# Recommendation tower in fp32: another order of the first loads, the row groups, the dense part and layer 3

## What is computed

```python
e = stack([tbl_f[ids[:, f]] for f in range(26)], axis=1)          # 512 x 26 x 128
combined = concatenate([dense[:, None, :], e], axis=1)            # 512 x 27 x 128
interactions = einsum('bfd,bgd->bfg', combined, combined)
z = concatenate([dense, interactions[:, iu, ju]], axis=1)         # 128 + 351
h = concatenate([z, dense], axis=1)
h = maximum(h @ W_top1 + b_top1, 0.0)                             # 607 -> 512
h = maximum(h @ W_top2 + b_top2, 0.0)                             # 512 -> 256
y = h @ W_top3                                                    # 256 -> 1
```

## Time and profile before

| | |
|---|---|
| median of 3 runs | 160.93 us (159.38 to 162.19) |
| profiled execution | 159.99 us, of which 158.3 us span of the instructions |
| busy, of the span | TensorE 123.5, weight loads 104.2, VectorE 78.0, ScalarE 73.6, GpSimd 76.3 us |
| TensorE's granted clock | 0.903 on the mean of the span |
| DMA | 5021 packets, 12.00 MB |

### The profile page before, as it was taken

One profiled execution on the slowest core, in us unless ns is written; L12 is line 12 of the kernel. 1 busy time (PEld: TensorE's weight loads), 2 busy tenths in 40 slices (PEclk: granted clock), 3 DMA queues, 4 the chain that ended last, 5 costly groups with the idle time before them and its releaser, 6 DMA issues.

```text
span 158.3 us, 2029 instructions
## 1 busy us (share of the span) xinstructions
PE 123.5 (78%) x748; PEld 104.2 (66%) x748; DVE 78.0 (49%) x152; ACT 73.6 (47%) x126; POOL 76.3 (48%) x73
## 2 busy tenths in 40 slices
PE   5699999996599699879950172079799979978894
PEld 5477778774477588679930160078599977977891
DVE  6698999897077878174100100038334502343331
ACT  3473999979507999451400100044624333335232
POOL 2779878778787888787777777000000000000000
PEclk9999999999659999999997555557999999999999
DMA  5864444576239811111111221000000000000000
GB/s 142 213 184 144 132 116 150 180 190 193 77 90 340 309 55 37 50 33 50 54 50 50 61 55 50 17 0 0 0 4 0 0 0 4 0 0 0 4 0 1
DMA packets 5021, 12.00 MB, mean 76 GB/s; under 512 B 1834, under 2 KB 2346, under 8 KB 4884
## 3 DMA queue, kind: packets, MB, share of 16 engines
q1 hardware_dynamic: 2800, 7.61, 15.7%
q0 software_dynamic: 2048, 4.20, 9.3%
q10 hardware_dynamic: 164, 0.07, 0.2%
HBM read 11.87 MB, written 0.00 MB: 75 GB/s over the span
## 4 chain that ended last, share of the span: by engine, by line
PE 38%; POOL 22%; another core or an unknown queue 16%; issue 7%; DMA 6%; DVE 5%; ACT 3%; ACTq 0%
POOL e_rows L342 22%; PE gram L428 13%; DMA e_rows<-in_tbl,idx 4%; PE gram L444 4%; PE late L399 3%; PE late L398 3%; PE look L408 2%; DVE dots L589 2%; PE late L462 2%; PE late L463 2%; PE late L464 2%; DMA idx<-in_ids_rows 2%; PE look L500 2%; DVE w_lo L842 1%
## 5 line engine op out<-in xcount | busy, mean ns | idle before, releaser
L342 POOL DMA_INDIRECT e_rows<-in_tbl,idx x64 | 75.4, 1179 | 21.7 <-issue 19.2
L428 PE MATMUL gram<-eT 128*123 128x104 f32 x256 | 33.3, 290 | 19.5 <-issue 11.5
L428 PEld LDWEIGHTS gram<-eT 128*123 128x123 f32 x256 | 31.6, 204 | 21.0 <-issue 12.5
L398 PE MATMUL late<-onehot,table_hi 125*128 125x512 f32 x86 | 37.4, 435 | 1.6 <-DVE onehot L760 1.6
L760 DVE TENSOR_SCALAR onehot<-ids,row_of_partition 125x512 fp32r<-125x512 f32 x73 | 31.6, 487 | 9.7 <-PE late L399 9.7
L399 PE MATMUL late<-onehot,table_lo 125*128 125x512 f32 x86 | 36.1, 420 | 0.0
L589 DVE COPY dots<-gram 32x208 f32<-32x208 f32 (+1 forms) x32 | 12.0, 376 | 40.8 <-remote 26.1
L612 ACT ACTIVATE dots<-gram 32x208 f32<-32x208 f32 x32 | 10.6, 333 | 43.1 <-remote 25.2
L398 PEld LDWEIGHTS late<-onehot,table_hi 125*128 125x128 f32 x86 | 18.0, 209 | 6.0 <-issue 2.3
L399 PEld LDWEIGHTS late<-onehot,table_lo 125*128 125x128 f32 x86 | 17.9, 208 | 3.6
L612 ACT ACTIVATE table_hi<-table 125x1024 fp32r<-125x1024 f32 (+2 forms) x11 | 11.4, 1039 | 14.7 <-PE late L399 11.5
(11 more groups left out here) (56 smaller groups left out, 122.8 us busy)
## 6 DMA issues: line engine op xcount, KB each, us to landing
table<-in_tbl SPq DMA_DIRECT2D x6, 448.0 KB
table<-in_tbl SPq DMA_DIRECT2D x3, 560.0 KB
w_raw<-in_w SPq DMA_DIRECT2D x1, 1280.0 KB
e_rows<-in_tbl,idx POOLq DMA_INDIRECT x64
w_raw<-in_w SPq DMA_DIRECT2D x1, 512.0 KB
table<-in_tbl SPq DMA_DIRECT2D x2, 224.0 KB
table<-in_tbl SPq DMA_DIRECT2D x6, 52.0 KB
x_rows<-in_dense SPq DMA_DIRECT2D x1, 256.0 KB
```

Of the source, the lines that this page charges most:

```text
L342: pool.indirect_dma_start(out=e_rows[:, t % 2, s, :], out_offset=None, in_=tables[f][:, :], in_offset=bass.IndirectOffsetOnAxis(ap=idx[:, ...
L398: pe.matmul(bank, table_hi[0:KP, i % 2, c, :], hot, start=c == 0, stop=False)
L428: last = pe.matmul(gram[0:ROWS_OUT, n % 2, q, 0:QUADS * NG_COL], eT_flat[:, b * SLOTS:b * SLOTS + ROWS_OUT], eT[:, b:b + QUADS, 0:NG_COL], ...
```

## The change

It has these parts.

- ScalarE issues the load of `ids_hot` ahead of that of `idx`. VectorE's memset of the pads is moved from its first place to the round of table 8. VectorE makes one one-hot instead of two before the first piece of `split_lo(0)`, and two between the pieces. Six warm-up matmuls instead of seven, and five more (`STAY_WARM`) behind the three spreads.
- Groups are turned one table later (`FIRST_TABLE` 2): (0, 0) behind table 2, and so on to (1, 2) behind table 8; behind table 9 none. Group (1, 3) is turned behind chunk 0 of gram_tile(0), (2, 0) and (2, 1) behind chunks 0 and 2 of gram_tile(1), (3, 0) and (3, 1) behind chunks 0 and 2 of gram_tile(2), (2, 2) behind the pairs, (2, 3) behind the turn.
- SyncE issues the loads of w1, w2, b2 and w3 after table 8's product. `w_sum` stands behind VectorE's copies of chunk 0 of tile 0, the split of w1's high part behind ScalarE's copies of chunk 1, the low part in two halves behind chunk 3 of tile 0 and chunk 0 of tile 1, and w2's high part behind chunk 1 of tile 1.
- layer1_dense(0) follows gram_tile(1). layer1_dense(1) is cut in two, one ahead of gram_tile(3), one behind it.
- layer3(0) stands between turn_pairs(1, 1) and turn_pairs(1, 2), writes to a bank of `gram` instead of `late`, with a semaphore of its own, and its copy follows `turn_lo(1)`.

```diff
-WARM_UP = 7
+W1_LO = [(0, 3), (1, 0)]
+WARM_UP, STAY_WARM = 6, 5
...
-FIRST_TABLE = 1
-EARLY = ALL_GROUPS[:NOH - FIRST_TABLE]
+FIRST_TABLE = 2
+EARLY = ALL_GROUPS[:NOH - FIRST_TABLE - 1]
+def early_groups(i):
+    return EARLY[i - FIRST_TABLE:i - FIRST_TABLE + 1] if i >= FIRST_TABLE else []
...
-BESIDE_GRAM = {0: REST[1][:NCH], 1: [None, REST[2][0], None, REST[2][1]],
-               2: [None, REST[3][0], None, REST[3][1]], 3: []}
+BESIDE_GRAM = {0: REST[1][:NCH], 1: [REST[2][0], None, REST[2][1]],
+               2: [REST[3][0], None, REST[3][1]], 3: []}
...
                 if i == NOH - 1:
+                    wait_late_full(sp, ("table", NOH - 2))
                     sp.dma_start(w1_raw[:, :, :], w1).then_inc(w_in, 16)
...
             def layer3(h):
-                bank = late_bank(("layer3", h))
+                if h == 0:
+                    wait_pairs_done(pe, 1, Y0_BANK)
+                bank = y0_bank if h == 0 else late_bank(("layer3", h))
...
+            for _ in range(STAY_WARM):
+                pe.matmul(gram[:, 1, 4, :], ident[:, :], ident[:, :], start=True, stop=True)
             for i in range(NOH):
                 one_hot_product(i)
                 spread_ids(i + IDS_AHEAD + 1)
-                if i >= FIRST_TABLE:
-                    turn_group(*EARLY[i - FIRST_TABLE])
-                else:
+                if i == 0:
                     turn_dense()
+                groups(early_groups(i))
             groups(BEFORE_GRAM[0])
             gram_tile(0)
             groups(BEFORE_GRAM[1])
-            layer1_dense(0)
             gram_tile(1)
+            layer1_dense(0, 0)
+            layer1_dense(0, 1)
             pairs_half(0)
...
-            groups(AFTER_LAYER2)
-            layer3(0)
-            groups(AFTER_LAYER3)
-            layer1_dense(1)
-            groups(BEFORE_GRAM[3])
-            gram_tile(3)
-            pairs_half(1)
-            for k in range(KT):
-                turn_pairs(1, k)
+            groups(AFTER_LAYER2 + AFTER_LAYER3 + BEFORE_GRAM[3])
+            layer1_dense(1, 0)
+            gram_tile(3)
+            layer1_dense(1, 1)
+            pairs_half(1)
+            for k in range(KT - 1):
+                turn_pairs(1, k)
+            layer3(0)
+            turn_pairs(1, KT - 1)
...
+            act.dma_start(ids_in_sb[:, :], ids_hot).then_inc(ids_in, 16)
             act.dma_start(idx[:, :, :], ids_rows).then_inc(idx_in, 16)
-            act.dma_start(ids_in_sb[:, :], ids_hot).then_inc(ids_in, 16)
...
-            act.wait_ge(w_in, 16 * 4)
-            act.wait_ge(w_sum, 1)
-            copy(w1_hi[:, :, :], w1_raw[:, 0:K1, :]).then_inc(w_hi, 1)
...
                     groups([k for k in BESIDE_GRAM[t][c:c + 1] if k])
+                    if (t, c) == (0, 1):
+                        act.wait_ge(w_sum, 1)
+                        copy(w1_hi[:, :, :], w1_raw[:, 0:K1, :]).then_inc(w_hi, 1)
+                    if (t, c) == (1, 1):
+                        copy(w2_hi[:, :, :], w2_raw[:, :, :]).then_inc(w_hi, 1)
...
-            dve.memset(eT[:, :, NF:SLOTS], 0.0).then_inc(pads_ready, 1)
...
-            one_hots(0, mine[:2])
-            split_lo(0)
-            one_hots(0, mine[2:])
+            one_hots(0, mine[:1])
+            split_lo(0, 0)
+            one_hots(0, mine[1:3])
+            split_lo(0, 1)
+            one_hots(0, mine[3:])
...
+                groups(early_groups(i - 1))
+                if i == NOH - 2:
+                    dve.memset(eT[:, :, NF:SLOTS], 0.0).then_inc(pads_ready, 1)
...
                     groups([k for k in BESIDE_GRAM[t][c:c + 1] if k])
+                    if (t, c) == (0, 0):
+                        dve.wait_ge(w_in, 16 * 4)
+                        dve.tensor_tensor(w1_raw[:, KT, :], w1_raw[:, KT, :], w1_raw[:, KT + 1, :], ALU.add
+                                          ).then_inc(w_sum, 1)
+                    if (t, c) in W1_LO:
+                        dve.wait_ge(w_hi, 1)
+                        k = slice(W1_LO.index((t, c)) * K1 // 2, (W1_LO.index((t, c)) + 1) * K1 // 2)
+                        dve.tensor_tensor(w1_lo[:, k, :], w1_raw[:, k, :], w1_hi[:, k, :].bitcast(F32), ALU.subtract
+                                          ).then_inc(w_lo, 1)
```

More of the change, by code:

```diff
@@ L131 @@
 LOOK = {what: n for n, what in enumerate(LOOK_ORDER)}
-assert FIRST_TABLE == 1 and all(("group", *k) in LOOK for k in ALL_GROUPS)
+assert all(("group", *k) in LOOK for k in ALL_GROUPS)
 def look_on_act(what):
@@ L464, in layer1_tile, with layer1_dense @@
                 return pe.matmul(o, w1_lo[:, k, rows], hi, start=False, stop=last_one, skip_group_check=True)
-            def layer1_dense(h):
+            def layer1_dense(h, i):
                 if h == 0:
                     pe.wait_ge(w_hi, 1)
-                    pe.wait_ge(w_lo, 1)
+                    pe.wait_ge(w_lo, len(W1_LO))
                 cols = slice(h * HB, (h + 1) * HB)
[L471 to L474, removed]
+                bank = late_bank(("layer1", h, i))
+                for n in (2 * i, 2 * i + 1):
+                    layer1_tile(bank, n, KT, x_hi[:, cols], x_lo[:, cols], n % 2 == 0, False)
             def layer1_pairs(h):
@@ L518, in layer3 @@
                     last = pe.matmul(bank[0:1, 0:HB], w3_sb[:, k:k + 1], h2[:, k, :], start=k == 0, stop=k == N2 - 1)
-                last.then_inc(late_full, 1)
+                last.then_inc(y0_full if h == 0 else late_full, 1)
             def groups(ks):
@@ L676, in _ @@
                     table_copy(i - 1)
[L677 to L678 removed]
+                groups(early_groups(i - 1))
             table_copy(NOH - 1)
[L680 to L684 removed]
+            groups(early_groups(NOH - 1))
             def dots_tile(t):
@@ L727, in _ @@
             dots_tile(0)
-            copy(w2_hi[:, :, :], w2_raw[:, :, :]).then_inc(w_hi, 1)
             groups(BEFORE_GRAM[1])
@@ L748, in _, with split_lo @@
             copy = dve.tensor_copy
-            def split_lo(i):
-                for a, c in PIECES[i]:
+            def split_lo(i, piece=0):
+                for a, c in PIECES[i][piece:piece + 1]:
                     dve.wait_ge(hi_ready, pieces_split(i, a))
@@ L796, in _ @@
                                       ALU.subtract).then_inc(look_dve, 1)
-                if i - 1 >= FIRST_TABLE:
-                    groups([EARLY[i - 1 - FIRST_TABLE]])
-            dve.wait_ge(w_in, 16 * 4)
-            dve.tensor_tensor(w1_raw[:, KT, :], w1_raw[:, KT, :], w1_raw[:, KT + 1, :], ALU.add
-                              ).then_inc(w_sum, 1)
-            groups(EARLY[-1:])
+                groups(early_groups(i - 1))
+                if i == NOH - 2:
+                    dve.memset(eT[:, :, NF:SLOTS], 0.0).then_inc(pads_ready, 1)
+            groups(early_groups(NOH - 1))
             def dots_tile(t):
@@ L836, in y_copy @@
             def y_copy(h):
-                wait_late_full(dve, ("layer3", h))
-                copy(y[0:1, h * HB:(h + 1) * HB], late[0:1, LATE["layer3", h] % 2, 0:HB]).then_inc(late_dve, 1)
+                if h == 0:
+                    dve.wait_ge(y0_full, 1)
+                    copy(y[0:1, 0:HB], y0_bank[0:1, 0:HB])
+                else:
+                    wait_late_full(dve, ("layer3", h))
+                    copy(y[0:1, h * HB:(h + 1) * HB], late[0:1, LATE["layer3", h] % 2, 0:HB]).then_inc(late_dve, 1)
             groups(BEFORE_GRAM[0])
-            dve.wait_ge(w_hi, 1)
-            dve.tensor_tensor(w1_lo[:, :, :], w1_raw[:, 0:K1, :], w1_hi[:, :, :].bitcast(F32), ALU.subtract
-                              ).then_inc(w_lo, 1)
             dots_tile(0)
@@ L856, in _ @@
             dots_tile(2)
-            groups(AFTER_LAYER2)
-            y_copy(0)
-            groups(AFTER_LAYER3 + BEFORE_GRAM[3])
+            groups(AFTER_LAYER2 + AFTER_LAYER3 + BEFORE_GRAM[3])
             dots_tile(3)
@@ L862, in _ @@
             turn_lo(1)
+            y_copy(0)
             h1_rest(1)
```

13 lines of the change are left out of this document (7 added, 6 removed).

## The result

| | kernel before | changed kernel |
|---|---|---|
| median, same set of runs | 160.42 us (159.38 to 162.19) | 164.4 us (164.06 to 165.94) |
| profiled execution, span | 159.99, 158.3 us | 165.94, 164.2 us |
| granted clock, mean | 0.903 | 0.875 |

The ratio is 1.029, with a 95% interval of 1.019 to 1.039: 4 us slower. The forecast was 150, and the range ended at 163. Further on, the same two kernels are found at 135.8 and 126.3 us, in another set of runs. Both pairs of numbers belong to the result; the hold lies between them: 24.6 and 38.1 us of time, where VectorE stands behind a remote releaser for 26.1 and 37.3 us.

The account below looks back on a forecast made before the run. TensorE was taken as the bound, busy 123.5 of 158.3 us, with a 22 us hold. Terms -0.8 -6.2 -1.2 +0.4 -2.8 = -10.6 took the median 160.93 to 150.3, forecast 150; range 127 to 163.

Parts of the forecast that it names:

- the hold: Around gram_tile(1): TensorE's matmuls started in time but seen complete late, VectorE's copies behind a remote releaser; 22 us, cause unknown.
- Front: Before and around the first product: filling TensorE's idle stretch may raise the clock earlier; -0.8 us (0 to -1.6).
- Groups: Table loop: turning groups one table later removes transposes' waits for rows and half-clock time; -6.2 us (-2 to -6.7).
- Table 9's copy: Before gram_tile(0): no transposes left behind table 9's product to cover the copy waited for; +0.4 us.
- Weights: gram_tile(0): moved w1 splits remove TensorE's wait before the third chunk, later load hidden by its lead; -1.2 us.
- Memset: Pads memset moved to VectorE's last but one round: nothing on the path, 0 to 2.2 us on GpSimd's gathers.
- Tail: From gram_tile(1) on: re-ordered groups, dense parts and layer 3 fill waits; -2.8 us (-1.5 to -2.8).
- A: The forecast: the hold comes again about as long, near 22 us, ending before 98; 150 us, chance 0.38.
- B: The hold ends with the gathers, within 1 us of 103.3, swallowing earlier gains; 160 us, chance 0.23.
- C: No hold, because work around gram_tile(1) is re-ordered; 22 us more go, 128 us, chance 0.21.
- D: The hold takes every chunk of the tile, 13.40 us each; 163.7 for three, 177 for four; chance 0.10.
- E: Table loop: waits for rows only move on, so the groups' 6.2 us are not won; 156 us, chance 0.08.

Follow-up runs that it names:

- e7: Kernel before with a 400-column GpSimd memset ahead of each gather of tiles 2 and 3; 136.7 us, kernel before 136.2.
- e9: Changed kernel with a 64-column GpSimd memset ahead of each gather of tiles 2 and 3; 127.9 us, kernel before 135.8.
- e8: Changed kernel as it is, run again in another set; 126.3 us against 135.8 for the kernel before, ratio 0.927.
- e2: Changed kernel without the 16 gathers of tile 3, its transposes reading tile 1's old rows; 141.7 us, one execution.
- e3: Changed kernel with the gathers of tile 3 put off until the transposes of group (2, 2) are done; 160.6 us.
- e16: Changed kernel with a 400-column GpSimd memset ahead of each gather of tiles 2 and 3; 137.6 us, kernel before 172.5.
- e18: Changed kernel with a 256-column memset ahead of each gather of tiles 2 and 3, w1's load and w_sum and high-part split later; 135.1 us, ratio 0.843.
- e1: Kernel before without the 16 gathers of tile 3, its transposes reading tile 1's old rows; 150.9 us, one execution.
- e12: Kernel before, unchanged, run again for its trace; 167.9 us.
- e13: Changed kernel with each group's gathers from tile 2 on waiting for the transposes one tile back, not two; 148.9 us.
- e14: Kernel before with only the change's order from gram_tile(1) on; 164.8 us (158.4 to 170.1).
- e15: Changed kernel with gathers from tile 2 on waiting for the transposes one tile back, run again; 148.2 us, kernel before 172.5.
- e17: Kernel before with only the change's order from gram_tile(1) on, run again; 159.4 us, kernel before 172.5.
- e4: Changed kernel with an unused 1024-column VectorE subtraction ahead of each chunk wait of tiles 0 and 1; 169.6 us, one execution.

## Why the prediction was wrong

**The sum was near.** It had 10.6 us, and without the hold the change is worth 9.5. Stages by the starts of their first matmuls, in traces without the hold (e7 for the kernel before, e9 for the changed one; each has its pauses in the gathers, and e7 a wait of 0.63 for rows in the last stage):

| stage | before | changed | difference | forecast |
|---|---|---|---|---|
| first product to gram_tile(0) | 56.9 | 52.0 | -4.9 | -6.6 |
| gram_tile(0) to pairs_half(0) | 18.3 | 17.2 | -1.1 | -1.2 |
| pairs_half(0) to layer2(0) | 19.4 | 19.9 | +0.5 | -1.2 |
| layer2(0) to the end | 31.1 | 29.3 | -1.8 | -1.6 |

From the first product on these two executions are 7.3 us apart, the medians of e8's set 9.5. The first stage ends before any hold in the two first traces as well, and there it is 58.4 and 52.0, -6.4.

*Front:* the rise of the clock came as said. The first product stands at 8.29 (8.20 before) and products are 0.23 us apart from 9.6 on. It is given back one table later: table 2's first product waits for a copy, and the clock is at 0.50 from 19.7 to 23.1. The term took no look at what is late next.

```profile
19.16 0.50 PE L411 MATMUL late<-onehot,table_hi 125*128 125x512 f32 x1 [1.34 <-ACT eT L628]
```

*Groups:* no transposes wait for rows and the half clock from 40.6 is gone, as said; 4.6 instead of 6.2 in the one run that undoes it. *Table 9's copy:* 1.11 before gram_tile(0), where e7 has 0.68: +0.4, as said. *Weights:* the 1.24 before the third chunk are gone (e9, timeline of TensorE), but the load's new place sometimes costs 6.04 us at (1, 2), where the prediction had "its rows should be there" and, at worst, nothing won:

```profile
62.65 7.60 PE L449 MATMUL gram<-eT 128*123 128x104 f32 x64
```

*Memset:* VectorE's memset at 55.43 lies beside gathers of 0.94 us and costs them nothing. The Trainium skill ("GPSIMD Engine Reference", Specifications) lets the two engines collide where VectorE's instruction has two SBUF inputs or runs in a two-port mode; by that rule, with a memset that has no input, the trace agrees.

```profile
55.67 0.94 POOL L354 DMA_INDIRECT e_rows<-in_tbl,idx  x1 [0.30 <-issue]
56.92 0.94 POOL L354 DMA_INDIRECT e_rows<-in_tbl,idx  x1 [0.30 <-issue]
```

*Tail:* the 1.28 before layer 2 are gone, the waits of 0.95 and 1.16 are 0.22 each. From layer 2 to the end it is 29.3 instead of 30.5 in the two first traces, -1.1 for -1.6. What was missed is the stage before it: two groups now stand around the turn, and layer 1 behind its short waits runs 3.2 us at half clock, which cost about what the removed wait gave. The window of the changed kernel; the kernel before had 1.00 in the same work (115.4 to 118.6):

```profile
122.20:125.40 3.20, 3.20 (x17) 3.20 (x16) 0.00 (x0) 0.17 (x1) 0.00 (x0) 0.50 0.00 0
```

**The hold decided, and its rival was mis-worked.** The step of the forecast that failed is "With the hold as long as it is": A took the hold for about 22 us of fixed length that moves forward with TensorE's program and ends before 98. Measured, it is 40 us and ends at 102.38, because its end goes with the last gather and not with the program (e2), and its start came 14 us earlier. B had the mechanism and the place: release within 1 us of 103.3, measured 102.38, and 103.31 for the next chunk. Its own step that failed is "What remains after it: 54.5 us now (158.3 less 103.8), plus dense(0) at half clock". That took it for granted that TensorE would have come as far by then as before. But the hold started 14 us earlier: the records show the four chunks of gram_tile(0) and nothing of gram_tile(1). What was on the near side of the release moved to the far one. From the release to pairs_half(0) are 11.7 us instead of 4.6, then +0.4 and -1.1: 60.9 instead of 54.5. Less the 0.5 by which the release is earlier, that is the 5.9 us of the two spans.

Why earlier: in the kernel before, gathers of 1.18 to 2.65 us stood between those of 0.94 up to 69, beside one-hots and the low part of w1, and the unbroken row of 0.94 begins at 71.7; TensorE was held from about 77. In the changed kernel VectorE is done with one-hots sooner and its 2.29 us are moved, the unbroken row begins at 55.67, and the transposes at 62.11 are the first to be seen late. In e3 TensorE's records come singly from 104.57 on, 10 us after the gathers begin anew at 94.59. The order in time is shown, and that slower gathers prevent it (e16, e18); that it is the row's length which starts it is argued from these.

In e1 the gathers from 53.5 to 61.6 take 0.95 to 1.16 us and start 1.25 to 1.46 apart, and TensorE is late from 62.5 on all the same. So a strictly unbroken row isn't needed, and the pace alone, 1.44 in e18, doesn't draw a clean line either.

C, with its 21 in 100, is right where the condition is absent: 126.3 for 128, but with the hold gone for the kernel before as well, and so not by the re-ordering that C gave as its reason. D's sign, over 35 us behind remote releasers, came, and its 163.7 for three held chunks lies near 164.4; that is luck, since 13.40 a chunk is not a constant of the chunk (24.1 us lie between the copies of chunk 0 and chunk 1 here) and the end is set by the gathers. E fell: with the groups one table on, the waits didn't move.

## What to carry to other kernels

Where a wait has a releaser that the profile can't name, beside a long row of indirect DMAs, space the DMAs out once before anything else is tuned. Here a memset of 0.33 or 0.45 us ahead of each gather went with 135.1 and 137.6 us instead of 164.4 for the changed kernel, in different sets under the condition. It isn't free: without the condition the longer one cost 11 us. A gain ahead of a stall with a fixed end is no gain, and can be a loss: what it lets the stall catch earlier is left to do behind it. Where the time of a baseline differs between sets of runs, measure the change in both conditions before it is judged.

## What the runs showed of the hardware

- While GpSimd issues gathers every 1.25 us or little more, TensorE's progress can be held, with nothing in the profile as releaser: in e3 records 0.7 us apart and more for 0.11, in the first trace of the kernel before 13.40 us between the copies of two chunks, where a chunk takes 1.83. At the end two chunks are seen done within 0.8 us, so at least a part of it is work whose end is seen late. Its main stretch goes on 3.2 to 5.1 us after the start of the last gather, or of the last one before a pause, in nine traces (before, e1, e2, e3, e12 to e15, e17), 6.0 in e4 and 6.8 in the changed kernel's first trace. In that one there is no DMA traffic from 98 to 102. One-hot products, transposes and gram matmuls were all hit. VectorE and ScalarE were idle through it and resumed at the same time as each other; whether they would have been slow as well isn't shown.
- The same kernel on the same chip takes 136 or 160 to 172 us by a condition that lasts for a set of runs. Under it single executions of the kernel before lie between 158 and 176 us; in e12 the hold's place had moved.
- A gather of 128 rows is 0.94 us beside a quiet VectorE and up to 4.00 beside a busy one.
- Open: what in the chip is shared; what the condition is; whether the matmuls are slow or only their ends are seen late; what starts the hold; and whether an empty pause does what the memset does, since every pause here was a memset.
